# Second GAT layer as weights on the count matrix in place of its edge pass, and a later start of the edge attributes' copy

## The chip, the core and the metric

The program runs on one core of a Trainium2 chip. The core has a matrix engine (PE), a vector engine (DVE), a scalar engine (ACT) and GpSimd (POOL), each with its own in-order instruction queue, and SP, which here only issues DMAs. The metric is the time of one execution on the device in microseconds.

## The reference, cut

3125 nodes of 128 features, 50000 edges sorted by destination. Four layers, each `x = x + layer(relu(norm(x)))`: a GCN, a transformer attention layer, two GAT layers (3 heads, then 1), and two SAGE layers. The change concerns the second GAT layer:

```python
feat = (h @ fc_w.T).reshape(n, heads, out_dim)
el = jnp.einsum('nhd,hd->nh', feat, attn_l)
er = jnp.einsum('nhd,hd->nh', feat, attn_r)
e = jax.nn.leaky_relu(el[src] + er[dst], 0.2)
m = jax.ops.segment_max(e, dst, num_segments=n)
ex = jnp.exp(e - m[dst])
s = jax.ops.segment_sum(ex, dst, num_segments=n)
out = jax.ops.segment_sum((ex / s[dst])[:, :, None] * feat[src], dst, num_segments=n)
out = out + (h @ res_w.T).reshape(n, heads, out_dim) + bias[None, :, :]
```

## The kernel before

The nodes stand in 25 tiles of 128, worked through in seven turns (one tile, then six times four). The edges are padded to 392 blocks of 128, in 98 groups of four.

**Prologue** (to about 390 us). POOL gathers, for ten chunks of 128 "steps" (a step is one block of 128 edges and one group of four destination nodes that it holds), the steps' sources (L968) and destinations (L971). SP's queue begins with the padding of the edge attributes, then waits for POOL's `attr_go` (L976) and copies the 12.5 MB of edge attributes (L706); all weights (L669) and the sort's stores and loads (L744, L739) stand behind that in the same queue. DVE and PE make from the steps the count matrix: for each chunk, how often each of the 3200 source nodes stands in each step, split by which of the four nodes of the group the edge goes to, 128 x (25 x 4 x 128) in bf16, 3.2 MB a chunk, kept in HBM (`adj_hbm`). The GCN and both SAGE layers are matmuls with that matrix (L1491, L1603), and a "pick" that adds the steps of a group up (L1585).

**Edge passes** (`edge_pass`, for the attention layer and both GAT layers). Tables of rows are stored to HBM, and POOL gathers one row of 129 to 256 numbers for each edge, 128 to an instruction, 392 instructions to a pass (L1041). For a group of four blocks DVE forms the logits (L2321, L2334), the running maximum along equal destinations (L2344, L2350) and the weighted rows; PE sums them with a matrix of equal destinations (L1696). Behind the groups the segments that cross blocks are joined, and POOL gathers each node's result (L1050). Only seven to eight groups may be in flight (`BEHIND`, `RB`). Then DVE divides (L2530, L2541), adds the residual and normalizes, turn by turn.

All queues are written by hand; the order in each is the order in the code, and semaphores tie them. No scheduler moves anything.

```python
for n in range(NG):
    ...
    for k in range(GC):
        at = n * GC + k
        g.indirect_dma_start(out=row_b[:, n % RB, k, 0:row_tab[p].shape[1]], out_offset=None,
                             in_=row_tab[p],
                             in_offset=bass.IndirectOffsetOnAxis(ap=src_i[:, at:at + 1], axis=0))\
         .then_inc(rows_in.of(n), 16)
```

## Time and profile before

| | us |
|---|---|
| median of 3 runs | 2798.61 (2792.72 to 2805.59) |
| the profiled execution | 2798.99 |
| its span, first to last instruction | 2796.3 |
| second GAT layer, from its last table row (L2585) to the SAGE matmuls (L1603) | 588.6 |

Over the span PE is busy 1962.9 us, DVE 1395.3, POOL 1381.5 and ACT 964.2; TensorE's granted clock is 0.808 of full speed on average. POOL's row gathers are on 35% of the chain that ended last. A row of a timeline gives start, duration, engine, line, operation, output and inputs (`arena` and `_sb` names are SBUF, `ps` is PSUM). An fp32 matmul is recorded as two instructions.

### The profile page before, as it was taken

Reading aid. Unit: us, or ns where it says so; the run is one execution under the profiler, and the core shown is the slowest. Engines: PE = TensorE matmul, PEld = TensorE weight load, DVE = VectorE, ACT = ScalarE, POOL = GpSimd, SP = SyncE. Lnnn points to the kernel's source line nnn. Section 1 sums busy time; section 2 is a strip of 40 time slices with the busy share of each in tenths; the row PEclk is TensorE's granted clock in tenths of the full one; section 3 lists DMA queues with packets and bytes.
Section 4 is the critical chain, followed back from the end, with each engine's and each line's share of the span. In section 5 each row is a group of like instructions: output and inputs, shape, how many; then the busy total and the mean of one; then the engine's idle time right before and its main releaser. Section 6 shows DMA issues by size and latency. Waiting matters only on the chain.

```text
span 2796.3 us, 33506 instructions
## 1 busy us (share of the span) xinstructions
PE 1962.9 (70%) x10867; PEld 1362.9 (49%) x10867; DVE 1395.3 (50%) x3099; ACT 964.2 (34%) x2148; POOL 1381.5 (49%) x1417
## 2 busy tenths in 40 slices
PE   3288896498888885557777776844444445499998
PEld 2155664377777773433333333533333334266666
DVE  7588857377777765544444443422222223522414
ACT  3444424233333335634444442422222222301202
POOL 5000004677777754677777770567777773300000
PEclk9998998689999886778888886865555555799999
DMA  4678892589999961167777773335555553565461
GB/s 105 188 277 300 278 312 75 169 251 262 265 259 275 259 197 42 29 190 240 239 240 243 238 233 106 74 78 133 133 133 133 133 133 82 187 204 155 142 202 31
DMA packets 469164, 505.22 MB, mean 181 GB/s; under 512 B 103669, under 2 KB 426632, under 8 KB 467552
## 3 DMA queue, kind: packets, MB, share of 16 engines
q1 hardware_dynamic: 245740, 211.11, 25.8%
q10 hardware_dynamic: 172724, 176.76, 19.3%
q0 software_dynamic: 50528, 115.22, 16.5%
q8 instruction: 89, 1.46, 0.2%
q14 instruction: 83, 0.68, 0.1%
HBM read 288.69 MB, written 227.42 MB: 185 GB/s over the span
## 4 chain that ended last, share of the span: by engine, by line
POOL 39%; PE 22%; issue 16%; DVE 12%; DMA 8%; ACT 3%; SPq 0%; POOLq 0%; ACTq 0%; DVEq 0%
POOL arena L1041 35%; PE ps L1603 10%; DVE arena L2013 3%; DMA arena<-erank 3%; PE ps L1585 2%; PE ps L1696 2%; PE ps L1491 1%; PE ps L1874 1%; DMA arena<-edst,step_i 1%; POOL arena L968 1%; DMA arena<-t_attn,src_i 1%; PE ps L1722 1%; DVE arena L2483 1%; ACT arena L1072 1%; DVE same_b L2159 1%
## 5 line engine op out<-in xcount | busy, mean ns | idle before, releaser
L1072 ACT ACTIVATE arena<-ps 128x774 f32<-128x774 f32 (+8 forms) x689 | 492.8, 729 | 1146.2 <-PE ps L1696 652.1
L1041 POOL DMA_INDIRECT arena<-t_gat,src_i x784 | 740.5, 944 | 238.9 <-issue 236.8
L1696 PE MATMUL ps<-arena 128*128 128x136 f32 (+2 forms) x2352 | 691.3, 455 | 86.4 <-DVE arena L2373 83.5
L1696 PEld LDWEIGHTS ps<-arena 128*128 128x128 f32 x2352 | 462.6, 260 | 237.3 <-DVE arena L2373 117.0
L1041 POOL DMA_INDIRECT arena<-t_attn,src_i x392 | 382.4, 975 | 126.5 <-issue 113.9
L2321 DVE TENSOR_TENSOR z_b<-arena 128x12 f32<-128x12 f32 (+1 forms) x196 | 33.6, 171 | 595.4 <-DMA arena<-t_gat,src_i 588.1
L1603 PE MATMUL ps<-arena 128*128 128x384 bf16 x1850 | 305.0, 328 | 35.0 <-DVE rec L2530 32.5
L1654 PE MATMUL ps<-ident,logit 128*64 128x128 f32 (+2 forms) x147 | 48.2, 328 | 381.2 <-DVE logit L2334 313.3
L1603 PEld LDWEIGHTS ps<-arena 128*128 128x128 bf16 x1850 | 181.8, 98 | 158.0 <-issue 40.6
L2373 DVE TENSOR_TENSOR arena<-arena,ps 128x1536 f32<-128x1536 f32 (+1 forms) x196 | 229.9, 1215 | 1.6 <-ACT arena L1231 1.6
L1654 PEld LDWEIGHTS ps<-ident,logit 128*64 128x64 f32 (+2 forms) x147 | 14.2, 97 | 427.0 <-DVE logit L2334 353.7
L2013 DVE TENSOR_TENSOR arena<-arena 128x1024 bf16<-128x1024 bf16 (+1 forms) x344 | 205.8, 656 | 0.2 <-PE ps L1505 0.2
L998 POOL TENSOR_TENSOR arena<-arena,r_L_gnn_gamma 128x512 f32<-128x512 f32 (+1 forms) x7 | 8.1, 1153 | 379.0 <-ACT arena L1302 379.0
L1491 PE MATMUL ps<-arena 128*128 128x385 bf16 x925 | 185.0, 341 | 0.0
L2313 DVE TENSOR_TENSOR arena<-arena,ps 128x1024 f32<-128x1024 f32 x98 | 119.2, 1216 | 131.6 <-DMA arena<-t_attn,src_i 100.3
L1072 ACT ACTIVATE arena<-same_b 128x512 f32<-128x512 bf16 x294 | 167.7, 621 | 30.1 <-DMA same_b<-same_hbm 30.1
L1072 ACT ACTIVATE arena<-arena 128x512 bf16<-128x512 f32 (+4 forms) x208 | 63.9, 307 | 273.5 <-DVE arena L2626 246.5
L1505 PE MATMUL ps<-arena 128*128 128x100 bf16 x1176 | 89.1, 223 | 86.5 <-DVE arena L2013 86.3
L2626 DVE TENSOR_REDUCE arena<-ps 128x128 f32<-128x384 f32 x74 | 36.2, 551 | 220.0 <-PE ps L1603 220.0
L1505 PEld LDWEIGHTS ps<-arena 128*128 128x128 bf16 x1176 | 75.2, 106 | 114.3 <-DVE arena L2013 94.5
L1636 PE MATMUL ps<-w_e,arena 64*128 64x128 f32 x784 | 124.3, 304 | 0.0
L1646 PE MATMUL ps<-arena 128*128 128x128 f32 x784 | 123.6, 305 | 0.0
(323 smaller groups left out, 2579.2 us busy)
## 6 DMA issues: line engine op xcount, KB each, us to landing
ends_gat<-arena ACTq DMA_DIRECT2D x98, 774.0 KB
arena<-adj_hbm SPq DMA_DIRECT2D x90, 640.0 KB, 3.9
same_b<-same_hbm SPq DMA_DIRECT2D x294, 128.0 KB, 4.7
adj_hbm<-arena ACTq DMA_DIRECT2D x9, 3200.0 KB, 11.4
ends_attn<-arena ACTq DMA_DIRECT2D x98, 272.0 KB
ends_gat<-arena ACTq DMA_DIRECT2D x98, 258.0 KB
arena<-starts_q SPq DMA_DIRECT2D x98, 256.0 KB, 5.3
same_hbm<-same_b SPq DMA_DIRECT2D x98, 128.0 KB, 3.8
```

The costliest lines, as they stand in the source:

```text
L1041: g.indirect_dma_start(out=row_b[:, n % RB, k, 0:row_tab[p].shape[1]], out_offset=None, in_=row_tab[p], in_offset=bass.IndirectOffsetOnAxi ...
L1072: return a.activation(o, i, ACT.Copy)
L1491: i = mm(bank(4 + n % 4)[:, 0:3 * D + 1], lhs, xs0[:, t, 0:3 * D + 1], start=t == 0, stop=t == NT - 1)
L1505: i = mm(ps[:, at:at + KEYS], hot_e[:, b % 3, e // 2, :, e % 2], hot_k[:, b % 3, e // 2, :, e % 2], start=True, stop=True)
L1603: m = mm(bank(ch % 2 * 4 + dl)[:, 0:3 * D], ring[:, u % RING, at:at + P], xs1[:, t, :, :].rearrange("p s c -> p (s c)"), start=t == 0, sto ...
L1636: i = mm(bank((1, 6)[g % 2])[:, k * D:(k + 1) * D], at_t[:, g % 2, k * P:(k + 1) * P], w_e[:, :], start=True, stop=True)
L1646: i = mm(bank((3, 7)[g % 2])[:, k * D:(k + 1) * D], same_f[:, g % RB, k, :], q_b[:, g % UNROLL, k, :], start=True, stop=True)
L1654: nc.tensor.transpose(bank(TURN_BANK[p])[0:kh, 0:P], logit[:, i % 2, 0:kh], ident[:, :])\
L1696: i = mm(o, same_f[:, g % RB, k, :], msg[:, g % 4, k * W:(k + 1) * W], start=True, stop=True)
L2013: return tt(o, bc(iota_two[:, 0:parts, :].rearrange("p (a i) s -> p a i s", a=1), [P, n, parts, 2]), bc(values.rearrange("p (a i s) -> p a ...
L2313: tt(kv, kv, bc(bank((1, 6)[g % 2]).rearrange("p (k s c) -> p k s c", k=GC, s=1), [P, GC, 2, D]), ALU.add).then_inc(kve_done.sem, 1)
L2373: tt(m[:, :, 0:heads * nc_].rearrange("p k (h c) -> p k h c", h=heads), rows_v, e, ALU.mult).then_inc(msg_done.sem, 1)
```

## The change

**First part.** The pass over the edges for the second GAT layer is gone (`edge_pass("gat2")` on all engines), with its tables of rows, starts and ends. In its place every pair of a source and a step gets a weight, from the count matrix: with `z = el[src] + er[dst]`, leaky ReLU is `0.2 z + relu(0.8 z)`. The matrix is streamed in ten chunks (`CHUNKS`: the short one of 32 steps first), 25 source tiles each, so 250 units of 128x512 numbers (the first 25 of 128x128). In each unit ACT makes `relu(0.8 er + 0.8 el)` (L1508), POOL adds the row `0.2 er - m` (L1173), ACT takes the exponential with `0.2 el` added (L1515, to PSUM), DVE multiplies by the counts (L3034) and PE multiplies the four 128x128 weights with the source tile's features and a column of ones (L2060, four fp32 matmuls of 129 columns), accumulating in PSUM over the 25 tiles.

The maximum `m` of a step is needed before its weights: `look` (L2915) takes, one source tile after another, `max(acc, min(count, y))` with `y` a scaled `el`. The 25 looks of a chunk stand in the first 17 slots (`LOOK_BY`) of the chunk before it. At slots 15 to 22 PE turns the result, DVE makes the maxima (L2937 to L2946), PE spreads them over the partitions, and DVE copies the row (L2952). The rings: 4 log tiles, 3 PSUM banks, 3 weight tiles, 2 chunks of counts (loaded by SP in five pieces of 640 KB). In the last chunk DVE also joins the steps' maxima per group of nodes (two scans of 1184 columns, `merged`) and writes the selection matrices. Behind the chunks come factors, denominators, eight picks per group of nodes as in the first layer (L1585), their transposes, and the norm without division and the product and addition ahead of it. The table of `er` is stored by ACT, and POOL gathers it for ten chunks (L1163).

**Second part.** POOL raises `attr_go` behind its memset and after all step gathers have landed, not before. SP's copy of the edge attributes waits for it.

```diff
+CHUNKS = [NC - 1] + list(range(NC - 1))
+PIECE2 = 5
+ONE = D + 1
+LOOK_BY = 17
+TOP = 1.0e30
...
-            edge_pass("gat2")
+
+            def load_piece(i, q):
+                n = PIECE2 * wide(i)
+                sp.dma_start(adj2[i % 2][:, q * n:(q + 1) * n], adj_hbm[CHUNKS[i], :, q * n:(q + 1) * n])\
+                  .then_inc(adj2_in[i % 2 * (NT // PIECE2) + q].sem, 16)
+
+            for i in range(NC):
+                if i < 2:
+                    sp.wait_ge(pe_o.sem, pe_o.at("gat1", ("tr", "lin")[i]))
+                for q in range(NT // PIECE2):
+                    if i >= 2:
+                        sp.wait_ge(*w_done.at((i - 2) * NT + ((q + 1) * PIECE2 if i > 2 else NT)))
+                    load_piece(i, q)
...
-            sp.wait_ge(s_steps, chains["x_gat2"].end)
+            sp.wait_ge(pe_o.sem, pe_o.at("gat2", "tr"))
...
+            g.memset(xs0[:, :, 3 * D:XW], 1.0).then_inc(s_ones, 1)
+            pool.wait_ge(step_edges, 16 * 2 * SOON)
+            pool.wait_ge(late_edges, 16 * 2 * (NC - SOON))
             pool.sem_inc(attr_go, 1)
-            g.memset(xs0[:, :, 3 * D:XW], 1.0).then_inc(s_ones, 1)
...
-            for j in range(NJ):
-                pool.wait_ge(feat_out, TURNS[j][1])
-                scatter("gat2", j)
-            edge_pass("gat2")
+
+            pool.wait_ge(*idx2_done.at(1))
+            pool.wait_ge(*er_out.at(16 * NJ))
+            for ch in CHUNKS:
+                g.indirect_dma_start(out=er_g[:, ch, :], out_offset=None,
+                                     in_=er_tab["gat2"].rearrange("(g d) c -> g (d c)", d=DG),
+                                     in_offset=bass.IndirectOffsetOnAxis(ap=step_i[:, 0, ch:ch + 1], axis=0))\
+                 .then_inc((er_first if ch == NC - 1 else er_rest).sem, 16)
+            for n in range(NC * NT):
+                i = n // NT
+                if n % NT == 0:
+                    pool.wait_ge(*dve_2.at("row_b", i))
+                pool.wait_ge(*relu2_done.at(n + 1))
+                z = log_b[:, n % 4, 0:wide(i)]
+                gt(z, z, row_b2[:, i % 2, 0:wide(i)], ALU.add).then_inc(sum2_done.sem, 1)
...
-            edge_pass("gat2")
+            for j in range(NJ):
+                act.wait_ge(feat_out, TURNS[j][1])
+                act.dma_start(er_tab["gat2"][TURNS[j][0] * P:TURNS[j][1] * P, :].rearrange("(k p) c -> p k c", p=P),
+                              tiles(er_all["gat2"], j)).then_inc(er_out.sem, 16)
...
+            def relus(n):
+                i, t = n // NT, n % NT
+                if t == 0:
+                    act.wait_ge(*act_2.at("row_a", i))
+                if n >= 4:
+                    act.wait_ge(*exp2_done.at(n - 3))
+                a.activation(log_b[:, n % 4, 0:wide(i)], row_a[:, i % 2, 0:wide(i)], ACT.Relu, bias=el8[:, t:t + 1])                    .then_inc(relu2_done.sem, 1)
+
+            def exps2(n):
+                i, t = n // NT, n % NT
+                act.wait_ge(*sum2_done.at(n + 1))
+                if n >= 3:
+                    act.wait_ge(*w_done.at(n - 2))
+                a.activation(bank((2, 4, 0)[n % 3])[:, 0:wide(i)], log_b[:, n % 4, 0:wide(i)], ACT.Exp,
+                             bias=el2[:, t:t + 1]).then_inc(exp2_done.sem, 1)
...
+            for n in range(NC * NT + 2):
+                if n % NT == 12 and n // NT < NC - 1:
+                    row_kept(n // NT + 1)
+                if n < NC * NT:
+                    relus(n)
+                if n >= 2:
+                    exps2(n - 2)
...
-            edge_pass("gat2")
...
+            def rows_a(i):
+                pe.wait_ge(*dve_2.at("er9" if i == 0 else "er"))
+                if i >= 1:
+                    pe.wait_ge(*dve_2.at("row_b", i - 1))
+                spread_rows(i, r_a[:, CHUNKS[i], :], pe_2.sem)
+
+            def look_turned(i):
+                pe.wait_ge(*look_done.at((i + 1) * NT))
+                pe.wait_ge(*act_2.at("row_a", i))
+                for dl in range(wide(i) // P):
+                    m = nc.tensor.transpose(part(bank(1), dl), part(acc, dl), ident[:, :])
+                m.then_inc(pe_2.sem, 1)
+
+            def rows_b(i):
+                pe.wait_ge(*dve_2.at("m", i))
+                spread_rows(i, r_b, pe_2.sem)
+
+            def products(i, t):
+                n = i * NT + t
+                pe.wait_ge(*w_done.at(n + 1))
+                if t == 0 and i >= 2:
+                    pe.wait_ge(*out2_read.at(i - 1))
+                for dl in range(wide(i) // P):
+                    m = mm(out2(i, dl), part(w_b[:, n % 3, :], dl), tab_gat1[:, t, :], start=t == 0 and dl in (0, DG - 1),
+                           stop=t == NT - 1, skip_group_check=True)
+                m.then_inc(out2_done.sem, 1)
...
+            for i in range(NC):
+                for t in range(NT):
+                    products(i, t)
+                    if i < NC - 1:
+                        if t == 6:
+                            rows_a(i + 1)
+                        elif t == LOOK_BY - 2:
+                            look_turned(i + 1)
+                        elif t == LOOK_BY:
+                            rows_b(i + 1)
...
-            edge_pass("gat2")
...
+            def look(i, t):
+                w = wide(i)
+                if t % PIECE2 == 0:
+                    dve.wait_ge(*adj2_at(i, t))
+                if t == 0:
+                    if i >= 1:
+                        dve.wait_ge(*pe_2.at("look", i - 1))
+                    k = ts(acc[:, 0:w], adj2_of(i, t), y_el[:, t:t + 1], None, ALU.min)
+                else:
+                    dve.wait_ge(*look_done.at(i * NT + t))
+                    k = stt(acc[:, 0:w], adj2_of(i, t), y_el[:, t:t + 1], acc[:, 0:w], ALU.min, ALU.max)
+                k.then_inc(look_done.sem, 1)
...
+            def maxima2(i):
+                ch, k = CHUNKS[i], wide(i) // P
+                if i >= 1:
+                    dve.wait_ge(*pe_2.at("rows_b", i - 1))
+                dve.wait_ge(*pe_2.at("look", i))
+                did(v.reduce_max(m_c[:, 0:k], bank(1)[:, 0:k * P].rearrange("p (d s) -> p d s", s=P), axis=AX_X))
+                settled()
+                did(ts(m_c[:, 0:k], m_c[:, 0:k], rng[:, 0:1], c2[:, 1:2], ALU.mult, ALU.subtract))
+                settled()
+                e, m = er_s[:, ch, 0:k], m_all[:, ch, 0:k]
+                did(tt(m_z[:, 0:k], m_c[:, 0:k], e, ALU.add))
+                settled()
+                did(stt(m, m_z[:, 0:k], 0.2, m_z[:, 0:k], ALU.mult, ALU.max))
+                settled()
+                stt(r_b[:, 0:k], e, 0.2, m, ALU.mult, ALU.subtract).then_inc(dve_2.sem, 1)
+
+            def row_copied(i):
+                dve.wait_ge(*pe_2.at("rows_b", i))
+                if i >= 2:
+                    dve.wait_ge(*sum2_done.at((i - 1) * NT))
+                v.tensor_copy(row_b2[:, i % 2, 0:wide(i)], bank(1)[:, 0:wide(i)]).then_inc(dve_2.sem, 1)
...
+            for i in range(NC):
+                for t in range(NT):
+                    n = i * NT + t
+                    if i < NC - 1 and t < LOOK_BY:
+                        for k in range(t * NT // LOOK_BY, (t + 1) * NT // LOOK_BY):
+                            look(i + 1, k)
+                    if t == 2 and i >= 1:
+                        taken(i - 1)
+                    dve.wait_ge(*exp2_done.at(n + 1))
+                    if t % PIECE2 == 0:
+                        dve.wait_ge(*adj2_at(i, t))
+                    if n >= 3:
+                        dve.wait_ge(*out2_done.at(n - 2))
+                    stt(w_b[:, n % 3, 0:wide(i)], bank((2, 4, 0)[n % 3])[:, 0:wide(i)], TOP, adj2_of(i, t), ALU.min, ALU.mult)                        .then_inc(w_done.sem, 1)
+                    if i < NC - 1:
+                        if t == LOOK_BY + 2:
+                            maxima2(i + 1)
+                        elif t == LOOK_BY + 5:
+                            row_copied(i + 1)
...
-            in_turns(dve_o, "gat2", **weighted("gat2"),
-                     yr=by_turn(dve_o, "gat2", "num", lambda j: tiles(agg_of("gat2"), j)[:, :, 0:D],
-                                lambda j: tiles(agg_of("gat2"), j)[:, :, 0:D], on(h_sb), ALU.add),
-                     xad=by_turn(dve_o, "gat2", "yr", on(x_sb), lambda j: tiles(agg_of("gat2"), j)[:, :, 0:D], on(x_sb), ALU.add),
+            def added(j):
+                dve.wait_ge(*y2_done.at(j + 1))
+                tt(tiles(x_sb, j), tiles(y_gat2, j), tiles(x_sb, j), ALU.add).then_inc(dve_o.sem, 1)
+
+            in_turns(dve_o, "gat2", xad=added,
```

POOL's queue from the end of the first GAT layer to its own end. Before, L1041 being the row gathers and L1050 the gathers of results:

```order
L1041 DMA arena<-t_gat,src_i 128x131 x392
L1050 DMA arena<-ends_gat,end_i 128x387 x25
L990 DMA starts_er<-er_all,start_i 53376x2 x25
L1028 DMA arena<-er_gat,first_i 98x2 x4
L1041 DMA arena<-t_gat,src_i 128x129 x392
L1050 DMA arena<-ends_gat,end_i 128x129 x25
```

And after (L1138 and L1147 are the old L1041 and L1050):

```order
L1138 DMA arena<-t_gat,src_i 128x131 x392
L1147 DMA arena<-ends_gat,end_i 128x387 x25
L1163 DMA arena<-er_gat,step_i 128x8 x10
L1173 TENSOR_TENSOR arena<-arena 128x128 x25
L1173 TENSOR_TENSOR arena<-arena 128x512 x225
```

The last 446 DMAs of POOL's queue are replaced by 10 and 250 additions.

DVE's queue in the second GAT layer. Before, in the loop over groups (L2373 weighs rows, L2344 and L2350 are the scans):

```order
L2373 TENSOR_TENSOR arena<-arena,ps 128x4x128 x2
L2344 SCALAR_TENSOR_TENSOR arena<-arena,ps 8x128
L2350 SCALAR_TENSOR_TENSOR arena<-arena 8x128
L2321 TENSOR_TENSOR z_b<-arena 128x4
L2334 SCALAR_TENSOR_TENSOR logit<-z_b 128x4
```

And after, in a full chunk from slot 15 to slot 22 (L2915 looks, L3034 products with the counts):

```order
L2915 SCALAR_TENSOR_TENSOR arena<-arena 128x512
L3034 SCALAR_TENSOR_TENSOR arena<-ps,arena 128x512
L2915 SCALAR_TENSOR_TENSOR arena<-arena 128x512 x2
L3034 SCALAR_TENSOR_TENSOR arena<-ps,arena 128x512 x4
L2937 TENSOR_REDUCE arena<-ps 128x4
L2939 TENSOR_SCALAR arena<-arena 128x4
L2942 TENSOR_TENSOR arena<-arena 128x4
L2944 SCALAR_TENSOR_TENSOR arena<-arena 128x4
L2946 SCALAR_TENSOR_TENSOR arena<-arena 128x4
L3034 SCALAR_TENSOR_TENSOR arena<-ps,arena 128x512 x3
L2952 COPY arena<-ps 128x512
```

DVE's work is now two kinds of wide operations; the small chain of maxima stands behind the fourth product that follows the last look.

## Rows read from the trace of the kernel before

**Rows 1.** By stretch: bounds, length, busy us (count) per engine, clock, DMA share.

```profile
780.00:1200.00 420.00, 312.83 (x1899) 258.69 (x1897) 272.01 (x590) 175.41 (x387) 271.53 (x275) 0.81 0.63 174
...
1830.00:2230.00 400.00, 176.78 (x684) 144.85 (x682) 106.31 (x359) 100.99 (x300) 299.18 (x315) 0.57 0.54 127
```

**Rows 2.** Chain of waits at both ends of the stage: start us, us, what.

```profile
1840.29 0.21 DVE h_sb L2585
...
1840.91 5.23 DMA er_gat<-er_all
...
2429.14 20.96 PE ps L1603 x128
```

**Rows 3.** Groups, 2000 to 2040 us: shapes; busy us, mean ns; idle before.

```profile
L1041 POOL DMA_INDIRECT arena<-t_gat,src_i x33 | 31.1, 943 | 10.1 <-issue 10.1
```

**Rows 4.** Timeline (start us, us, engine, line, operation) around 474 us.

```profile
473.57 1.28 POOL L998 TENSOR_TENSOR arena<-arena,r_L_gnn_gamma 128x512 f32<-128x512 f32 x1
473.74 0.68 DVE L2483 TENSOR_TENSOR h_sb<-ps,h_sb 128x512 f32<-128x512 f32 x1
...
474.34 1.08 DVE L2483 TENSOR_TENSOR arena<-arena,r_L_gnn_b 128x512 f32<-128x512 f32 x1
```

**Rows 5.** Timeline around 1114 us, POOL and DVE.

```profile
1114.01 1.26 POOL L998 TENSOR_TENSOR arena<-arena,r_L_gnn_g 128x512 f32<-128x512 f32 x1 [8.00 <-ACT arena L1302]
...
1114.36 1.46 DVE L2541 TENSOR_TENSOR arena<-arena,rec 128x512 f32<-128x512 f32 x1
...
1115.35 1.59 POOL L1005 TENSOR_TENSOR arena<-arena,r_L_gnn_b 128x512 f32<-128x512 f32 x1
```

**Rows 6.** Timelines of DVE and POOL where the other does not interfere.

```profile
466.29 0.68 DVE L2483 TENSOR_TENSOR arena<-arena,r_L_gnn_b 128x512 f32<-128x512 f32 x1
...
492.45 1.28 POOL L998 TENSOR_TENSOR arena<-arena,r_L_gnn_gamma 128x512 f32<-128x512 f32 x1
```

**Rows 7.** DVE by group, ACT by line, PE from two timelines.

```profile
L2373 DVE TENSOR_TENSOR arena<-arena,ps 128x512 f32<-128x512 f32 x8 | 5.1, 681 | 0.0
...
L1373 ACT ACTIVATE arena<-ps,b1c x42: 361/690/716, 1750.1 to 1828.1; 128x512 f32<-128x512 f32 x36, 128x128 f32<-128x128 f32 x6
...
2018.20 2.09 PE L1696 MATMUL ps<-arena 128*128 128x129 f32 x8
...
2589.00 1.06 PE L1889 MATMUL ps<-sage_t,ht 128*128 128x128 f32 x8
```

**Rows 8.** The two scans over 392 columns, by line: min/median/max ns.

```profile
L2433 DVE TENSOR_TENSOR_SCAN arena<-arena x2: 961/968/974, 2370.5 to 2373.8; 1x392 f32<-1x392 f32 x1, 128x392 f32<-128x392 f32 x1
```

**Rows 9.** Timeline of PE at the end of the first layer.

```profile
399.71 11.68 PE L1585 MATMUL ps<-arena 128*128 128x128 f32 x56
411.33 5.84 PE L1546 MATMUL ps<-ones,arena 4*128 4x1 f32 x50
417.10 4.50 PE L1585 MATMUL ps<-arena 128*128 128x121 f32 x14
...
421.89 8.79 PE L1585 MATMUL ps<-arena 128*128 128x121 f32 x42
```

**Rows 10.** Timeline of DVE: starts of two turns of the norm's pipeline.

```profile
2402.26 0.17 DVE L2530 TENSOR_SCALAR rec<-arena 128x4 f32<-128x4 f32 x1
...
2408.04 0.17 DVE L2530 TENSOR_SCALAR rec<-arena 128x4 f32<-128x4 f32 x1
```

**Rows 11.** The first 160 us: chain of waits, then SP's queue.

```profile
74.11 30.87 DMA arena<-edst,step_i
...
58.05 0.51 SPq L706 DMA_DIRECT2D eattr<-in_edge_attr  x1
...
63.85 29.44 SPq L669 DMA_DIRECT2D r_L_gnn_b<-in_L_gnn_b  x1
...
122.16 1.55 SPq L669 DMA_DIRECT2D ends_gat<-zrow  x2
147.94 0.32 SPq L744 DMA_DIRECT2D same_hbm<-same_b  x1
```

More of the change, by code:

```diff
@@ L34 @@
 UNROLL = 4
[L35 removed]
+WEIGHTED = {"attn": (H1, C1, 0.25), "gat1": (H2, D, 1.0)}
 PASSES = tuple(WEIGHTED)
@@ new lines, in group_rows, with max_rows @@
+            def group_rows():
+                pe.wait_ge(*out2_read.at(NC - 1))
+                for ch in range(NC):
+                    o = rows2(0, ch)
+                    m = mm(o, bc(step_f[:, 2, ch:ch + 1], [P, DG]), ident[:, 0:o.shape[1]], start=True, stop=True)
+                m.then_inc(pe_2.sem, 1)
+            def max_rows():
+                pe.wait_ge(*dve_2.at("read"))
+                for ch in range(NC - 1):
+                    nc.tensor.transpose(rows2(1, ch), m_all[:, ch, :], ident[:, :])
+                mm(rows2(1, NC - 1), mask[:, :], m_r9[:, :], start=True, stop=True).then_inc(pe_2.sem, 1)
@@ new lines, in factors @@
+            def factors():
+                pe.wait_ge(*act_2.at("f"))
+                pe.wait_ge(*dve_2.at("fg"))
+                for ch in range(NC - 1):
+                    nc.tensor.transpose(bank(1)[:, ch * DG:(ch + 1) * DG], part(m_r, ch), ident[0:DG, 0:DG])
+                mm(bank(1)[:, (NC - 1) * DG:(NC - 1) * DG + 1], f_g[:, :, :].rearrange("d e s -> d (e s)"), ones[0:DG, 0:1],
+                   start=True, stop=True).then_inc(pe_2.sem, 1)
+            rows_a(0)
+            look_turned(0)
@@ new lines, in denominators @@
+            def denominators():
+                for half in range(2):
+                    g0, g1 = half * HALF, (half + 1) * HALF
+                    use = [ch for ch in range(NC) if SPAN[ch][0] < g1 and SPAN[ch][1] > g0]
+                    for ch in use:
+                        a0, a1 = max(SPAN[ch][0], g0), min(SPAN[ch][1], g1)
+                        off = SPAN_AT[ch] - SPAN[ch][0]
+                        subs = [0] if ch < NC - 1 else list(range(DG))
+                        for d in subs:
+                            lhs = s_v[:, ch, :, D] if ch < NC - 1 else den9[:, :]
+                            m = mm(bank(2 + half)[0:DG, a0 - g0:a1 - g0], lhs,
+                                   sel2[:, off + d * ENDW + a0:off + d * ENDW + a1], start=ch == use[0],
+                                   stop=ch == use[-1] and d == subs[-1], skip_group_check=True)
+                m.then_inc(pe_2.sem, 1)
@@ L2592, in split1 @@
+            settled()
+            for j in range(NJ):
+                dve.wait_ge(pe_o.sem, pe_o.at("gat2", "tr", j))
+                for k, t in enumerate(range(*TURNS[j])):
+                    i = stt(y_gat2[:, t, :], part(bank(j), k), rec2[:, t:t + 1], h_sb[:, t, :], ALU.mult, ALU.add)
+                i.then_inc(y2_done.sem, 1)
             def split1(stage, after):
```

304 lines of the change are left out of this document (286 added, 18 removed).

## The prediction

> **What bounds the kernel now.** I read the page's chain of waits first; its largest part is POOL's row gathers. The table by stage [rows 1] then shows where PE, the largest engine of the page, is idle: from 1830 to 2230 us, inside the second GAT layer, PE is busy 177 of 400 us at a granted clock of 0.57 and DVE 106, while POOL is busy 299. The chain of waits through that stage says why. POOL issues one row gather after another, each 0.94 us plus 0.30 us of issue [rows 3], so 392 gathers cost 490 us, whatever PE and DVE do. The edges of the stage are the last row written by L2585 (ends at 1840.5) and the start of the SAGE matmuls behind L2603 at 2429.1 [rows 2], from where PE doesn't stop. So the change trades 2429.1 - 1840.5 = **588.6 us**, and the rest of the kernel stands, but for the first 160 us.
>
> **The new stage, part by part.** Of the 588.6 us, 490 go with the row gathers, and with them the 25 scatters, 4 first gathers and 25 result gathers. In place of them stand 250 units: ten chunks of 25 source tiles, the chunk of 32 steps first (128 columns wide), then nine of 512 columns.
>
> One full unit is, on each engine:
> - ACT: a Relu with a per-row bias and an Exp with another, each 128x512. The nearest row is L1373, 0.69 us alone [rows 7] and about 0.60 when they follow each other; 1.2 to 1.3 us a unit.
> - POOL: one add of two SBUF tiles, 1.28 us in L998 when DVE leaves it alone [rows 6].
> - DVE: the product of Exp (PSUM) and counts (SBUF), 0.68 us by L2373, which has the same kinds of operands [rows 7]; in a row they follow at 0.60. And in the first 17 of 25 slots 25 "looks" at the next chunk, each with two SBUF inputs: 0.68 us alone by L2483 [rows 6].
> - PE: four fp32 products of 129 columns, recorded as 8 instructions. L1696 shows 2.09 us for 8 at the low clock, L1889 1.06 us for 8 of nearly the same width at the full one [rows 7]. So 25 units are 25 us of PE at 2.4 GHz and 50 us at 1.2 GHz.
>
> If these ran freely, a chunk's first 17 slots would be DVE's: 25 x 0.66 + 17 x 0.60 + 1.5 of small ones = 28.2 us, and the last 8 slots ACT's and POOL's at 1.29 = 10.3: 38.5 us a chunk.
>
> They don't run freely. POOL's L998 starts at 473.57 and lasts 1.28; DVE's L2483 with its PSUM operand goes through beside it in 0.68; but the next L2483, with two SBUF inputs, shows 1.08 us instead of 0.68 [rows 4]. The group at 1114 us has the whole exchange [rows 5]: POOL's L998 ends at 1115.27; DVE's L2541 (two SBUF inputs), begun at 1114.36, ends at 1115.82, 0.55 behind it; POOL's L1005, begun at 1115.35, ends at 1116.94, 1.12 behind that. So work of these two kinds alternates, and one pair takes 0.55 + 1.12 = 1.67 us. In the new loop every look and every add are such a pair of rivals. The Trainium skill has this as a rule (page "SBUF — State Buffer", section "SBUF: two separate sides"): a GpSimd instruction and a DVE one with two SBUF inputs need the same port pair, and whoever starts first keeps it for its whole length. By that rule a chunk is the sum worked out next and not the 38.5, so it speaks against the change; the trace agrees, 1.08 for 0.68.
>
> So in the looks' part I take the exclusive time: 25 looks x 0.55 = 13.8; and the adds that fall into it, 17 of its own and up to 4 more since POOL may run a ring of four ahead: 21 x 1.12 = 23.5; sum 37.3, and 2 for the copies of sums and rows between, 39.3. Behind it come 8 slots without looks. POOL has the four ahead, so ACT and the chain of maxima (PE turns, five small DVE operations, PE spreads, DVE copies) set them, 8 x 1.2 to 1.4 = 9.5 to 11. Together **c = 50 us a chunk**. If no look ever waits and POOL takes only 17 adds in that part, it is 13.8 + 17 x 1.12 + 10.3 = 43; if PE's waits in the maxima's part (it holds its queue for them at slot 17, while DVE may be only three units ahead) are not hidden, 5 to 6 are added, 56. I take 50, the case in which both rings are used as they are written, and keep 44 to 56.
>
> The whole stage then:
> - Lead, 18.4: the table's store lands 5.2 behind 1840.9 [rows 2], 0.4 ahead of it, and ten gathers at 1.25 [rows 3] stand in POOL's queue before its first add.
> - The short chunk, 29: 25 looks at the first full chunk (17) and 25 narrow products at an estimated 0.35 us (8.8), 3 for the chain of maxima.
> - 4.5 us: the third chunk's counts may be loaded only when the short chunk is through, and its looks wait; my estimate, somewhat over the four us that such a piece takes.
> - Eight full chunks with looks: 8 x 50 = 400.
> - The last chunk has no looks. POOL sets it, 25 x 1.28 = 32; the penalties, two scans over 1184 columns (0.97 us for 392 in L2433 [rows 8], so 2.9 each) and the selection matrices stand on DVE's queue beside it, of which I let 10 show: 42.
> - The tail. Scaling 7.5. The picks are written as the first layer's L1585 is, and cost the same columns: 11.68 + 4.50 + 8.79 = 25.0, with 5.8 of L1546 between them [rows 9]; denominators are a quarter of a pick set, 6.3; 3 for a clock that has fallen, 1 for the evacuation: 41. Then transposes, y and the norm's pipeline. Now that pipeline has a turn each 5.78 us (L2530 at 2402.26 and 2408.04 [rows 10]) and takes 42.7 from its first result (2386.3) to the end edge; without division, product and one add a turn is 1.75 shorter, six turns 10.5; transposes and y for all turns stand ahead, 9: 41. Sum 89.5.
>
> 18.4 + 29 + 4.5 + 400 + 42 + 89.5 = **583.4**, against 588.6: **5 us gained**. One us more or less in c is 8 us of the kernel.
>
> **The edge-attribute copy.** SP issues the 12.5 MB copy at 58.05 now, and POOL's step gathers run on until 74.11; the last one's data lands 30.9 us later, and DVE waits for it [rows 11]. With the copy behind the landing (about 3 us behind the last gather) DVE goes on at 77.5 and not 105.0: 27.5 us. But the copy stands at the head of SP's queue with all the weights behind it, and so the queue moves 19.5 us later. It is blocked 29.4 us by the copy now, and ends its loads at 122.16 + 1.55; then it ends near 143.3. The next that SP has to do is store and load of the sort (L744, at 147.94 now and some 120 if DVE were alone). DVE's sort waits for the fourth of those loads, now about 153.6, then 143.3 + 5.5. So 27.5 becomes **4.5 us**. Ends: 0, if the copy slows the sort's own loads; 25, if SP isn't blocked again.
>
> The sum is made on the profiled run, whose own time is 2798.99 (span 2796.3); the median shown, 2798.61, is the same to 0.4 us. 2799.0 - 5.2 - 4.5 = **2789.3 us**.
>
> **Rivals.**
> 1. The exclusion costs less, c = 44 (looks and adds fall into each other's gaps, and POOL doesn't use its lead). For it: 13.8 + 17 x 1.12 + 10.3. Against: the loop lets POOL start whenever a log tile is free. 8 x 6 = 48 less: 2741.
> 2. No exclusion in this mix, since the look's first operand is bf16: c = 38.5, 92 less: 2697. No row has that pair; [rows 4, 5] speak against it.
> 3. **Slower: TensorE at 1.2 GHz.** The stage now runs at 0.57 with PE half busy [rows 1]. If the clock stays there, PE needs 50 us a chunk, and as it stands idle 6 to 7 us for the maxima, c = 57: 8 x 7 = 56 more, 2845. It decides from where PE's own time, 25 x u and its idle 6.5, passes 50, which is u = 1.74 us a unit, a granted clock of about 0.6. For it: the clock that the present stage shows. Against: from 780 to 1200 us, with PE 74% busy, the clock is 0.81 [rows 1], and at c = 50 PE would be busy 60 to 75%.
> 4. The prologue gives all it could, 25 and not 4.5: 2769. SP's 29.4 us behind the copy speak against it.
> 5. The second part does nothing (the landing was late for another reason): 2794. The first can't fail to do what it says: 1176 row gathers become 784 by its text.
>
> **How the numbers follow.** Forecast with c from 47 to 54 (2765 to 2821): 0.48. Rival 1: 0.20. Rival 2: 0.08. Rival 3: 0.17. Rivals 4 and 5 by themselves: 0.05 and 0.02. A measurement tells 0.5%, 14 us, from no change: faster is below 2784.6, slower above 2812.6. Faster gets rivals 1, 2 and 4 and 0.09 of the forecast's, 0.42; slower rival 3 and 0.10 of the forecast's, 0.27; same the rest, 0.31. The range leaves out rival 2 and half of each outer slope: 2737 to 2845.
>
> **What would show it.** In the changed profile the stage from L2585's successor to the SAGE matmuls is 583 us, and eight stretches of 50 us repeat in it. POOL's L1173 shows a mean of about 1.5 us, not 1.28, and DVE's L2915 about 1 us, not 0.66, while L3034 stays at 0.68. If L1173 stays at 1.28 and L2915 at 0.68, the exclusion was wrong. If L2060 shows 8 instructions in 2.0 us nearly everywhere and DVE waits for it, rival 3 holds. DVE's L2033 starts near 77 and SP's L669 ends near 143. The forecast fails most easily on c, of which no row shows the whole, and on the tail, which is put together from three other stages.

## The result

| | before | after |
|---|---|---|
| median, us | 2802.1 (4 runs) | 2833.17 (2829.24 to 2838.12, 4 runs) |
| profiled execution, us (span) | 2798.99 (2796.3) | 2832.71 (2831.0) |

The changed kernel is slower: ratio 1.012, 95% interval 1.0104 to 1.0137. The forecast was 2789.3, a little faster, with a range to 2845; the time lies in the range and the sign is wrong: a gain of 10 us was forecast, a loss of 31 came. The page of the changed kernel, part 1 (busy us, share of the span, instructions):

```profile
PE 2138.7 (76%) x12214; PEld 1540.6 (54%) x12214; DVE 1738.4 (61%) x3276; ACT 1146.9 (41%) x2266; POOL 1306.9 (46%) x1231
```

PE is busy 176 us more than before, DVE 343 more, ACT 183 more, POOL 75 less: the change takes idle time out of the span and puts busy time in. Busy is not all work: an operation of DVE or POOL that waits for the other one counts as busy while it waits (a look shows 1.225 us below, of which 0.745 are its own). The page's costliest groups of the new loop (line, engine, operation, out<-in, count | busy, mean ns | idle before, releaser):

```profile
L2060 PE MATMUL ps<-arena 128*128 128x129 f32 x1850 | 326.1, 343 | 140.5 <-DVE arena L3034 138.6
L1173 POOL TENSOR_TENSOR arena<-arena 128x512 f32<-128x512 f32 (+1 forms) x250 | 347.9, 1418 | 171.0 <-ACT arena L1508 117.7
...
L2915 DVE SCALAR_TENSOR_TENSOR arena<-arena 128x512 f32<-128x512 bf16 (+1 forms) x240 | 273.0, 1138 | 4.3
...
L1515 ACT ACTIVATE ps<-arena 128x512 f32<-128x512 f32 (+1 forms) x250 | 163.4, 654 | 195.0 <-DVE arena L3034 167.3
...
L3034 DVE SCALAR_TENSOR_TENSOR arena<-ps,arena 128x512 f32<-128x512 f32 (+1 forms) x250 | 157.8, 641 | 50.7 <-PE ps L2060 40.0
```

The rows to compare with [rows 6] and [rows 7] are the looks, L2915, and POOL's additions, L1173. By shape, from 1840 to 2400 us:

```profile
L1173 POOL TENSOR_TENSOR arena<-arena 128x512 f32<-128x512 f32 x225 | 329.6, 1492 | 164.2 <-ACT arena L1508 111.2 <-DVE arena L2952 53.0
...
L2915 DVE SCALAR_TENSOR_TENSOR arena<-arena 128x512 f32<-128x512 bf16 x216 | 264.6, 1225 | 3.2
...
L3034 DVE SCALAR_TENSOR_TENSOR arena<-ps,arena 128x512 f32<-128x512 f32 x225 | 151.0, 681 | 45.2 <-PE ps L2060 36.5 <-ACT ps L1515 8.1
```

A look takes 1.225 us on average, an addition 1.492, and the product with its operand in PSUM 0.681, as before for L2373. The forecast had said about 1, about 1.5 and 0.68. That is the exchange of [rows 5]; not every look meets it (single ones below show 0.7 to 0.8 us).

**The account.** I lay the forecast's terms beside what the trace of the changed kernel has. The edges of the chunks are the starts of L2912, the first look of a chunk, and of L2952, the copied row: 1888.4, 1940.8, 1997.4, 2052.3, 2107.1, 2161.8, 2216.5, 2271.3, and by the same distance behind L2952 (1.8 us) 2326.1.

| term | forecast | measured | difference |
|---|---|---|---|
| ahead of the stage (1840.5 before, 1835.1 after) | -4.5 | -5.4 | -0.9 |
| lead, to POOL's first addition (1854.1) | 18.4 | 19.0 | +0.6 |
| short chunk and reload (1888.4) | 33.5 | 34.3 | +0.8 |
| eight chunks (2326.1) | 400 | 437.7 | **+37.7** |
| last chunk, to the end of DVE's last product with counts (2379.1) | 42 | 53.0 | **+11.0** |
| tail, to PE's unbroken SAGE matmuls (2452.5) | 89.5 | 73.4 | **-16.1** |
| behind that edge | 0 | 11.3 | **+11.3** |

The differences add up to 44.4, and the profiled run is 43.4 above the forecast (one us lies outside the span). The terms ahead of and behind the stage compare single profiled executions, and the executions of one kernel differ by up to 16 us here, so a difference of a few us in them is no finding by itself.

### The profile page after: what moved, and what is told of

It reads as the page before. It is cut to its first block, busy times and chain, and to the rows that moved or that the text cites. A ratio compares the mean times of both kernels' runs of the same rounds, so it can differ in the third digit from the quotient of the medians.

```text
span 2831.0 us, 35859 instructions
## 1 busy us (share of the span) xinstructions
PE 2138.7 (76%) x12214; PEld 1540.6 (54%) x12214; DVE 1738.4 (61%) x3276; ACT 1146.9 (41%) x2266; POOL 1306.9 (46%) x1231
## 3 DMA queue, kind: packets, MB, share of 16 engines
q0 software_dynamic: 36576, 87.66, 11.4%
## 4 chain that ended last, share of the span: by engine, by line
PE 26%; POOL 25%; DVE 19%; issue 17%; DMA 5%; ACT 3%; SPq 3%; POOLq 0%; DVEq 0%; ACTq 0%
POOL arena L1138 23%; PE ps L1750 11%; DVE arena L2915 6%; DMA arena<-erank 3%; PE ps L2060 3%; DVE arena L2292 3%; SPq L757 2%; DVE arena L3034 2%; PE ps L1732 2%; PE ps L2021 1%; PE ps L1843 1%; PE ps L1638 1%; PE ps L2145 1%; DVE arena L2762 1%; DVE same_b L2438 1%
## 5 line engine op out<-in xcount | busy, mean ns | idle before, releaser
L1180 ACT ACTIVATE arena<-ps 128x774 f32<-128x774 f32 (+6 forms) x601 | 439.6, 748 | 829.6 <-PE ps L1843 297.4
L1843 PE MATMUL ps<-arena 128*128 128x136 f32 (+1 forms) x1568 | 484.3, 461 | 71.3 <-DVE arena L2652 67.6
L1138 POOL DMA_INDIRECT arena<-t_attn,src_i x392 | 383.3, 978 | 127.6 <-issue 114.9
L2060 PE MATMUL ps<-arena 128*128 128x129 f32 x1850 | 326.1, 343 | 140.5 <-DVE arena L3034 138.6
L1173 POOL TENSOR_TENSOR arena<-arena 128x512 f32<-128x512 f32 (+1 forms) x250 | 347.9, 1418 | 171.0 <-ACT arena L1508 117.7
L1138 POOL DMA_INDIRECT arena<-t_gat,src_i x392 | 370.1, 944 | 119.5 <-issue 117.6
L2060 PEld LDWEIGHTS ps<-arena 128*128 128x128 f32 x1850 | 296.5, 249 | 168.1 <-DVE arena L3034 167.7
L2915 DVE SCALAR_TENSOR_TENSOR arena<-arena 128x512 f32<-128x512 bf16 (+1 forms) x240 | 273.0, 1138 | 4.3
L1515 ACT ACTIVATE ps<-arena 128x512 f32<-128x512 f32 (+1 forms) x250 | 163.4, 654 | 195.0 <-DVE arena L3034 167.3
L3034 DVE SCALAR_TENSOR_TENSOR arena<-ps,arena 128x512 f32<-128x512 f32 (+1 forms) x250 | 157.8, 641 | 50.7 <-PE ps L2060 40.0
L1508 ACT ACTIVATE arena<-arena 128x512 f32<-128x512 f32 (+1 forms) x250 | 168.6, 675 | 0.0
L2652 DVE TENSOR_TENSOR arena<-arena,ps 128x1536 f32<-128x1536 f32 x98 | 167.3, 1749 | 0.9 <-ACT arena L1339 0.9
L1180 ACT ACTIVATE arena<-arena 128x512 bf16<-128x512 f32 (+3 forms) x159 | 54.7, 344 | 273.1 <-DVE arena L3129 246.5
```

The source lines that it names most:

```text
L1173: gt(z, z, row_b2[:, i % 2, 0:wide(i)], ALU.add).then_inc(sum2_done.sem, 1)
L1180: return a.activation(o, i, ACT.Copy)
L1508: a.activation(log_b[:, n % 4, 0:wide(i)], row_a[:, i % 2, 0:wide(i)], ACT.Relu, bias=el8[:, t:t + 1]) .then_inc(relu2_done.sem, 1)
L1843: i = mm(o, same_f[:, g % RB, k, :], msg[:, g % 4, k * W:(k + 1) * W], start=True, stop=True)
L2060: m = mm(out2(i, dl), part(w_b[:, n % 3, :], dl), tab_gat1[:, t, :], start=t == 0 and dl in (0, DG - 1), stop=t == NT - 1, skip_group_chec ...
L2652: tt(m[:, :, 0:heads * nc_].rearrange("p k (h c) -> p k h c", h=heads), rows_v, e, ALU.mult).then_inc(msg_done.sem, 1)
```

## Where the time is in a chunk

From the timeline of DVE, the chunk that begins at 2107.07. The views' columns are start, duration, engine, line, operation:

```profile
2107.07 0.52 DVE L2912 TENSOR_SCALAR arena<-arena 128x512 f32<-128x512 bf16 x1
2108.07 0.69 DVE L3034 SCALAR_TENSOR_TENSOR arena<-ps,arena 128x512 f32<-128x512 f32 x1 [0.47 <-ACT ps L1515]
2108.68 1.82 DVE L2915 SCALAR_TENSOR_TENSOR arena<-arena 128x512 f32<-128x512 bf16 x1
2110.42 0.68 DVE L3034 SCALAR_TENSOR_TENSOR arena<-ps,arena 128x512 f32<-128x512 f32 x1
2111.03 2.82 DVE L2915 SCALAR_TENSOR_TENSOR arena<-arena 128x512 f32<-128x512 bf16 x2
```

and its end:

```profile
2146.02 2.42 DVE L2915 SCALAR_TENSOR_TENSOR arena<-arena 128x512 f32<-128x512 bf16 x2
2148.36 2.69 DVE L3034 SCALAR_TENSOR_TENSOR arena<-ps,arena 128x512 f32<-128x512 f32 x4
2150.97 0.68 DVE L2937 TENSOR_REDUCE arena<-ps 128x4 f32<-128x512 f32 x1
2151.69 1.37 DVE L2939 TENSOR_SCALAR arena<-arena 128x4 f32<-128x4 f32 x1
2153.09 1.19 DVE L2942 TENSOR_TENSOR arena<-arena 128x4 f32<-128x4 f32 x1
2154.32 0.16 DVE L2944 SCALAR_TENSOR_TENSOR arena<-arena 128x4 f32<-128x4 f32 x1
2154.51 0.16 DVE L2946 SCALAR_TENSOR_TENSOR arena<-arena 128x4 f32<-128x4 f32 x1
2154.62 0.69 DVE L3034 SCALAR_TENSOR_TENSOR arena<-ps,arena 128x512 f32<-128x512 f32 x1
2158.02 0.69 DVE L3034 SCALAR_TENSOR_TENSOR arena<-ps,arena 128x512 f32<-128x512 f32 x1 [2.71 <-PE ps L2060]
2159.43 0.69 DVE L3034 SCALAR_TENSOR_TENSOR arena<-ps,arena 128x512 f32<-128x512 f32 x1 [0.71 <-PE ps L2060]
2160.03 0.68 DVE L2952 COPY arena<-ps 128x512 f32<-128x512 f32 x1
...
2161.83 0.52 DVE L2912 TENSOR_SCALAR arena<-arena 128x512 f32<-128x512 bf16 x1
```

Two looks and the wait for the additions between them fill 2.82 us, where 1.5 would do. The part with looks ends at 2148.44 and is 41.4 us long (forecast 39.3). In this part DVE hardly pauses: the first look, 24 others at 1.29 us and 17 products at 0.60 fill it. POOL stands idle for 10.0 us of it, waiting for ACT, where the forecast's sum had a look or an addition at work all the time. The rest is 13.4 us, where I had 9.5 to 11. In it stand two things that the value I took leaves out: operations on four numbers a partition last 1.37 and 1.19 us (0.16 for the two right behind them), and DVE then waits 2.71 and 0.71 us for PE. PE's own rows show why:

```profile
2149.10 2.05 PE L2060 MATMUL ps<-arena 128*128 128x129 f32 x16
2154.73 1.46 PE L2034 MATMUL ps<-ident,arena 128*128 128x128 f32 x8 [3.58 <-DVE arena L2946]
2155.98 8.19 PE L2060 MATMUL ps<-arena 128*128 128x129 f32 x59
```

Its queue is held for 3.58 us by the spreading of the maxima (L2034), with the products of slots 18 and 19 behind it, and DVE may be only three units ahead.

## Experiments

Two theories. **A**: looks and additions exclude each other, and that carries the chunk. **B**: PE carries it, by its held queue or by TensorE's clock; this is the forecast's rival 3. Each run is timed beside the kernel before on the same chip (medians 2800.8 to 2803.5).

**POOL's addition left out** (the row 0.2 er - m is missing in the weights).

```diff
-                gt(z, z, row_b2[:, i % 2, 0:wide(i)], ALU.add).then_inc(sum2_done.sem, 1)
+                g.memset(z[:, 0:1], 0.0).then_inc(sum2_done.sem, 1)
```

> The changed kernel with POOL's addition (L1173) replaced by a memset of one column, so the row 0.2 er - m is left out of the weights and the output is not the reference's. Theory A (looks and additions exclude each other): the looks (L2915) fall from 1.225 us mean to 0.68, a chunk from 54.7 to about 40 us (25 x 0.66 + 17 x 0.60 + 1 for the looks' part, 12 behind it), the whole to about 2833 - 8 x 14.5 - 5 = 2712. Rival B (PE's queue, held for the maxima, or TensorE at a low clock sets the chunk): looks get shorter but DVE waits for PE or ACT instead, a chunk stays above 50, the whole above 2800.

Measured 2682.4 us (one run), a chunk 37.3 us. The looks by shape, 1840 to 2400 us:

```profile
L2915 DVE SCALAR_TENSOR_TENSOR arena<-arena 128x512 f32<-128x512 bf16 x216 | 160.9, 745 | 3.1
```

0.745 us instead of 1.225: the additions cost the looks 0.48 us each, and a look alone is 0.745, not the 0.68 of [rows 6]. Theory A's direction and size hold; the gain, 151 us, is above the 121 I wrote. Not all of it is the looks: the edit also takes POOL's own time away, and shortens three more things.

- The small operations L2939 and L2942 fall from 0.95 and 1.07 us on average to 0.29 and 0.16.
- DVE's wait for PE in the same window falls from 36.5 to 7.1 us, although PE still holds its queue at slot 17.
- The last chunk, which has no looks, takes 41.2 us and not 53.0. In it DVE's operations on tables in SBUF shrink, those with a single tensor as input (and one number per partition) among them. First the changed kernel, then this one:

```profile
2338.02 4.27 DVE L2971 TENSOR_SCALAR arena<-ident,arena 32x32 f32<-32x32 f32 x4
```

```profile
2200.62 0.97 DVE L2971 TENSOR_SCALAR arena<-ident,arena 32x32 f32<-32x32 f32 x4
```

**The running maximum in PSUM.** Same computation; a look has one SBUF input. The first look of a chunk (L2912) writes to PSUM as well, and the last one writes the result back to SBUF.

```diff
-                if n >= 3:
-                    act.wait_ge(*w_done.at(n - 2))
-                a.activation(bank((2, 4, 0)[n % 3])[:, 0:wide(i)], log_b[:, n % 4, 0:wide(i)], ACT.Exp,
+                if n >= 2:
+                    act.wait_ge(*w_done.at(n - 1))
+                a.activation(bank((2, 4)[n % 2])[:, 0:wide(i)], log_b[:, n % 4, 0:wide(i)], ACT.Exp,
...
-                    k = stt(acc[:, 0:w], adj2_of(i, t), y_el[:, t:t + 1], acc[:, 0:w], ALU.min, ALU.max)
+                    o = acc if t == NT - 1 else bank(0)
+                    k = stt(o[:, 0:w], adj2_of(i, t), y_el[:, t:t + 1], bank(0)[:, 0:w], ALU.min, ALU.max)
```

> The changed kernel with the looks' running maximum in PSUM instead of SBUF (the last look of a chunk writes it to SBUF), so a look has one SBUF input; in exchange the exponentials have two PSUM banks instead of three. Same computation. Theory A: the exclusion is only against operations with two SBUF inputs, so looks show 0.68 us and POOL's additions 1.28, a chunk is 40 to 42 us and the whole 2833 - 8 x 13.5 - 3 = 2722. Rival B (PE's hold or the clock sets the chunk): within 10 us of 2833. Rival C (any look of bf16 is excluded): looks stay near 1.2 us, about 2833 or more, since the ring is shorter.

Measured 2738.35 us, ratio to before 0.9774 (0.9754 to 0.9793). A chunk is 43.4 us. By shape, 1840 to 2400 us:

```profile
L1173 POOL TENSOR_TENSOR arena<-arena 128x512 f32<-128x512 f32 x225 | 284.0, 1282 | 119.6 <-ACT arena L1508 64.2 <-DVE arena L2953 54.5
...
L2916 DVE SCALAR_TENSOR_TENSOR ps<-arena,ps 128x512 f32<-128x512 bf16 x207 | 154.9, 748 | 2.8
```

Looks 0.748 and additions 1.282, both as if alone. No work was taken out of the kernel, the ring of the exponentials got shorter, and 95 us went with the second SBUF input of the looks. That is 16 us less than the 111 I expected: the chunk is 43.4 and not 40 to 42, and DVE waits for PE as long as before (36.8 us in the window, 36.5 in the changed kernel). Rival C is out: it isn't the bf16 input. B is out as the carrier, since PE does the same work. The Trainium skill's rule (page "SBUF — State Buffer", section "SBUF: two separate sides") limits the exclusion on DVE's side to operations with two SBUF inputs and to operations in a two-port mode; by that rule this edit frees looks and additions, and the trace agrees. L2971, L2939 and L2912 wait too, with a single tensor input, in SBUF; no run here tells whether a two-port mode is what makes them. The number per partition that they read besides isn't it, since the freed looks read one as well.

**PE's spreading of the maxima two slots later.**

```diff
-                        elif t == LOOK_BY:
+                        elif t == LOOK_BY + 2:
                             rows_b(i + 1)
```

> The changed kernel with PE's spreading of the maxima (L2034, waits for DVE's L2946) moved in PE's queue from behind slot 17's products to behind slot 19's. Same computation. Now PE holds its queue 3.6 us there and DVE then waits 2.7 + 0.7 us for it in each chunk. Theory: those 3.4 us go, 8 or 9 times: 2833 - 29 = 2804. Rival (POOL waits for the copied row, 6.5 us a chunk, and that row now comes later): what DVE gains, POOL gives back, and the time stays at 2833 or rises by up to 10.

Measured 2807.17 us, ratio 1.0018 (1.0006 to 1.0031); a chunk 51.6 us. 26 us gained where 29 was expected. DVE's waits ahead of its products in the new loop, 1840 to 2400 us, fall from 45.2 to 15.1 us. A part comes back in the first look of each chunk, L2912, which now meets an addition nearly every time and takes 1.37 us on average instead of 0.66:

```profile
L3034 DVE SCALAR_TENSOR_TENSOR arena<-ps,arena 128x512 f32<-128x512 f32 x225 | 150.1, 680 | 15.1 <-PE ps L2060 9.5 <-ACT ps L1515 4.3
...
L2912 DVE TENSOR_SCALAR arena<-arena 128x512 f32<-128x512 bf16 x9 | 12.3, 1365 | 4.3 <-DMA arena<-adj_hbm 4.3
```

Beside the additions the held queue costs 3.1 us a chunk, at nearly the same granted clock (0.75 in a chunk of the changed kernel, 0.77 here): the part of theory B that is true. Without the additions it costs little (7.1 us of waits in the run above), since PE holds its queue for the small operations, and it is these that wait for POOL. This edit alone brings the change back to within 0.2% of the kernel before.

**Both edits.** 

> Both same-computation edits together: running maximum in PSUM (which brought the changed kernel from 2833 to 2738, a chunk from 54.7 to 43.4 us) and PE's spreading of the maxima behind slot 19 (which alone took 3.1 us off a chunk). In the run with the maximum in PSUM DVE still waits 3.1 us for PE there in each chunk. If the two costs are separate they add up: a chunk of 40.2 us, 2738 - 8 x 3.1 = 2713. Rival: without the exclusion POOL's wait for the copied row (6.5 us a chunk, 54.5 us in all) is next in line and takes the gain back: 2730 or more.

Measured 2716.24 us, ratio 0.9706 (0.9682 to 0.973), a chunk 40.4 us. The two gains add up nearly (2713 expected), and POOL's wait for the copied row does not take them back: it falls from 54.5 to 27.9 us, so it was a follower.

**Both, and the small operations of the maxima by way of PSUM.** The tensor_scalar writes its output to PSUM, and the operations behind it take one input from there.

```diff
-                did(ts(m_c[:, 0:k], m_c[:, 0:k], rng[:, 0:1], c2[:, 1:2], ALU.mult, ALU.subtract))
+                p_c, p_z, p_m = (bank(1)[:, q * DG:q * DG + k] for q in range(3))
+                did(ts(p_c, m_c[:, 0:k], rng[:, 0:1], c2[:, 1:2], ALU.mult, ALU.subtract))
...
-                did(tt(m_z[:, 0:k], m_c[:, 0:k], e, ALU.add))
-                settled()
-                did(stt(m, m_z[:, 0:k], 0.2, m_z[:, 0:k], ALU.mult, ALU.max))
-                settled()
-                stt(r_b[:, 0:k], e, 0.2, m, ALU.mult, ALU.subtract).then_inc(dve_2.sem, 1)
+                did(tt(p_z, p_c, e, ALU.add))
+                did(tt(m_z[:, 0:k], p_c, e, ALU.add))
+                settled()
+                did(stt(p_m, p_z, 0.2, m_z[:, 0:k], ALU.mult, ALU.max))
+                settled()
+                did(v.tensor_copy(m, p_m))
+                stt(r_b[:, 0:k], e, 0.2, p_m, ALU.mult, ALU.subtract).then_inc(dve_2.sem, 1)
```

> As the kernel with both edits, and the small operations of the maxima (4 numbers a partition) take one of their inputs from PSUM each. In the changed kernel they show 0.95 and 1.07 us where 0.16 is what the same kind shows undisturbed, since they too wait for POOL's additions. Theory (exclusion holds for any size, so three of them cost 1 us each): about 2.5 us less a chunk, 2713 - 8 x 2.5 = 2693. Rival (POOL is what the chunk waits for by then, and gains nothing from a shorter chain): within 5 us of the kernel with both edits.

Measured 2687.22 us, ratio 0.9601 (0.9577 to 0.9624), a chunk 37.3 us. The small operations in the chunk from 2100 us on:

```profile
L2941 DVE TENSOR_SCALAR ps<-arena 128x4 f32<-128x4 f32 x1 | 0.3, 284 | 0.0
...
L2947 DVE SCALAR_TENSOR_TENSOR ps<-ps,arena 128x4 f32<-128x4 f32 x1 | 0.2, 171 | 0.0
L2944 DVE TENSOR_TENSOR ps<-ps,arena 128x4 f32<-128x4 f32 x1 | 0.2, 170 | 0.0
```

In the kernel with both edits three of the small operations wait, at 0.63, 1.09 and 1.07 us on average. Of the 3.1 us that a chunk loses here 1.9 are their own time, and 1.1 is DVE's wait for PE (16.2 us in the window, now 6.2), which stood waiting for them.

With the same computation this is 146 us below the changed kernel and 4% below the kernel before: the best version here, and 124 of those 146 us (95 and 29) came from edits that only free DVE's operations from POOL's additions. The chunk of 37.3 is also what the loop has without any POOL addition; DVE is busy 35.3 of it, and POOL's 31.2 us now run beside that. The last chunk was not freed, and no run did that.

**Half of PE's products left out** (two of four column groups in 23 of 25 tiles).

```diff
                 for dl in range(wide(i) // P):
+                    if dl in (1, 2) and 0 < t < NT - 1:
+                        continue
```

> The changed kernel with half of PE's products left out in 23 of 25 tiles (the output is not the reference's), so PE has about 12 instead of 25 units of work in a chunk. Forecast's rival 3 (PE's products at a low clock carry the chunk): the chunk falls well below 50 us and the whole by 50 or more, to about 2780. Theory A (looks and additions exclude each other, PE only shows behind its hold): only DVE's wait for PE in slots 20 to 22 shrinks, 2 to 3 us a chunk: about 2810.

Measured 2814.9 us (one run), a chunk 54.4 us instead of 54.7. By stretch (bounds, length, busy us and count of PE, PEld, DVE, ACT and POOL, clock, DMA share, GB/s), first the changed kernel, then this one:

```profile
2090.00:2140.00 50.00, 34.92 (x207) 32.13 (x208) 45.52 (x55) 31.08 (x49) 34.70 (x23) 0.77 0.21 67
```

```profile
2090.00:2140.00 50.00, 28.20 (x125) 23.70 (x123) 46.79 (x53) 29.94 (x47) 34.02 (x23) 0.60 0.17 53
```

PE has little more than half the products, and its clock is 0.60 instead of 0.77, so that its busy time falls by a fifth only, which makes this a weaker test than I had planned. DVE's and POOL's columns are nearly those of the changed kernel, and so is the chunk. Together with the maximum in PSUM, where the chunk lost 11.3 us with all of PE's products in place, it says that rival 3 isn't what happened: PE's rate doesn't carry the chunk. Of the 18 us that this single run is shorter, 6.7 are there ahead of the first chunk already (its first row copy at 1845.80 and not 1852.54), 6.6 lie in the chunks, and the rest behind them.

**The second part alone, and the change without it.** In the kernel before:

```diff
-            pool.sem_inc(attr_go, 1)
             g.memset(xs0[:, :, 3 * D:XW], 1.0).then_inc(s_ones, 1)
+            pool.wait_ge(step_edges, 16 * 2 * SOON)
+            pool.wait_ge(late_edges, 16 * 2 * (NC - SOON))
+            pool.sem_inc(attr_go, 1)
```

> The kernel before with the second part of the change alone: the edge attributes' copy is let go only when all step gathers have landed. In the changed kernel the first picks start at 394.0 us, in the kernel before at 399.7. Theory: these 5.7 us come from the second part alone and reach the end: about 5.5 us less than the kernel before (ratio 0.998), picks (L1585) near 394. Rival: they come from the smaller loads of the first part (two DMAs fewer in that queue): no change, picks at 399.7.

Measured 2796.73 us against 2803.51, ratio 0.9973 (0.996 to 0.9986). But its profiled execution (2800.9, one of its slower ones) starts the picks at 399.66, no earlier than the kernel before. The ratio speaks for a gain, that trace doesn't place it. So the opposite edit on the changed kernel:

> The changed kernel without the second part: the copy is let go ahead of the step gathers, as in the kernel before. If the second part is worth what the kernel before gained by it alone (ratio 0.9973, 7.6 us less), this is about 2840, and the first picks start at 399 to 400 instead of 393.4 to 396.8. If the picks' earlier start comes from the first part (fewer loads in the queue), they stay near 394 and the time at 2833.

Measured 2839.78 us, ratio 1.0148 (1.012 to 1.0177), beside 1.012 (1.0104 to 1.0137) for the changed kernel. The intervals overlap, so these times alone don't show a difference. PE's row ahead of the picks, where the changed kernel has it at 393.88:

```profile
401.99 0.23 PE L1664 MATMUL ps<-arena,vdeg 128*4 128x148 bf16 x1 [1.34 <-DVE arena L2450]
```

Seven profiles of kernels with both parts have it at 392.9 to 396.7, this one at 402.0. The start of the sort's first store on SP's queue divides the gain: 147.9 in the kernel before, 146.0 with the second part alone, 148.9 with the first part alone, and 142.7 to 144.4 with both. So the later copy moves the sort more together with the first part than alone. By the times the second part is worth about 7 us, clear of noise only in the kernel before; why the trace of that run shows none of it at the picks stays open.

## Why the prediction was wrong, step by step

- **What bounds the kernel before, and what goes**: right. The stage of 588.6 us is gone with its 392 gathers, and nothing else of it came back.
- **The exclusion of looks and additions**: the mechanism is shown (runs with the addition left out and with the maximum in PSUM), and its part of the chunk came out near the forecast, 41.4 us for 39.3. That closeness is in part luck. The forecast's sum has looks and additions at work without a pause, 13.8 + 23.5 us; in the trace POOL is idle for 10.0 us of this part, a look takes 1.29 us in it where I expected about 1, and it is DVE's queue of looks and products that fills it. A look's own time is 0.745 us, for which I had taken an fp32 row of 0.68; no run tells how much of the two us that is.
- **The failing step is the rest of the chunk**: "8 x 1.2 to 1.4 = 9.5 to 11" was 13.4. I had seen that PE holds its queue at slot 17 and kept 5 to 6 us for it at the upper end, but let it be hidden in the value I took. It is not: 3.1 us a chunk (spreading two slots later). And I took the small DVE operations in as "small", without asking whether they wait for POOL. In the changed kernel two of them do, 1.6 us a chunk by their means with and without the additions. With both edits in place three do, and freeing them took 3.1 us off the chunk (40.4 to 37.3). The hold and the small operations aren't two separate costs, since PE holds its queue for them: without the additions the hold stands where it was, and the chunk is 37.3 too. With the two us of the looks' part the miss in c is 4.7, and eight times that is the 37.7.
- **The last chunk** failed the same way, 53.0 us for 42. I let POOL set it and let 10 us of DVE's work show, at undisturbed prices. Without the additions it takes 41.2 (the run with the addition left out), and with the looks freed alone still 52.4: what waits there are tensor_scalar operations (four of L2971 take 4.27 us instead of 0.97, two of L2997 with 518 columns 2.31 instead of 0.87) and one of the two scans (3.50 us instead of 2.61).
- **The stage's end edge**: wrong, and hidden by a second error. I put it where PE's matmuls become unbroken. Before that edge the kernel before had done 80 of the SAGE matmuls in the gaps between the norm's turns, the changed kernel only 20. The chains of waits from there, of before and after:

```profile
2429.14 137.47 PE ps L1603 x845
```

```profile
2452.51 148.83 PE ps L1750 x905
```

60 matmuls more are 11.4 us. On the other side the tail was 16.1 us shorter than I had it, for the most part since PE goes unbroken when the norm still has three turns of 3.9 us to do; I had counted all seven. The two cancel but for 5 us. That the sum of all terms but the chunks comes within 7 us is luck of this kind. A stage must end at a point with the same work left in both kernels.
- **The tail's picks**: right. From the chain of waits of the changed kernel:

```profile
2386.33 7.96 PE ps L2115 x34
2394.29 11.59 PE ps L2145 x56
2405.89 8.61 PE ps L2124 x50
2414.50 13.49 PE ps L2145 x56
```

11.6 + 13.5 = 25.1 against the 25.0 taken from [rows 9]; the small matmuls between took 8.6 and not 5.8, the denominators 8.0 and not 6.3. With the 3 us added for a fallen clock, which no row shows, the forecast's 41 meets the 41.7 from the denominators to the last pick.
- **The edge-attribute copy**: right in mechanism, and the size fits. The gathers' last landing takes 2.8 us instead of 30.9 [rows 11], SP's queue is blocked behind the copy as before and lets the sort's store through only at 143.3:

```profile
70.55 2.77 DMA arena<-edst,step_i
...
80.97 28.16 SPq L757
...
143.25 0.48 SPq L832
```

5.4 us of the 27.5 arrive at the start of the stage in the profiled executions, 4.5 was forecast. That is with both parts in place; with the second part alone the sort's first store moved by 2.0 us only, and not by the 4.7 seen here.
- **Rival 3** (TensorE's clock) had 0.17 and isn't what happened; its price was near what came, for another reason. **Rivals 1 and 2** fell: c is above, not below 50. **Rivals 4 and 5** fell as well: not all of the 25 us arrived, and not nothing. The forecast's own band for c, 47 to 54, ends just below the 54.7 that came.

## What to carry to other kernels

Before a loop puts GpSimd and DVE side by side, list each DVE operation, wide or of four numbers, that works on SBUF alone. Here those with two inputs in SBUF waited for the GpSimd operation under way, and so did tensor_scalar operations with a single tensor input, as long as their output was in SBUF too. Moving one input, or the output of a tensor_scalar, to PSUM removed that wait for the price of one PSUM bank, and (with a shorter hold of PE's queue) turned a loss of 1% into a gain of 4%. And price the chain that a held queue waits for with these waits in it. In a hand-written queue put an instruction that waits for a chain behind the work that doesn't, as far as the ring of buffers allows. And compare two kernels' stages only at points with equal work left.
